# Scores of a head pair in two PSUM banks, and the second FFN matmul three slots later

## The reference

```python
def attn_layer(x, Wqkv, qs, ksc, Wo):            # 16 heads of 64, windows of 32 tokens
    q, k, v = jnp.split(x @ Wqkv, 3, -1)         # each split into heads
    q = l2norm(q) * qs; k = l2norm(k) * ksc      # then rotary, with a scale by position
    sim = jnp.einsum('bhwie,bhwje->bhwij', bq, bk2) * 8.0   # a window against itself and the one before
    attn = jax.nn.softmax(jnp.where(mask, -big, sim), -1)
    return jnp.einsum('bhwij,bhwje->bhwie', attn, bv2) @ Wo

def ffn_layer(x, g, bln, W1, b1, W2, b2):        # inner width 341
    xn = layernorm(x) * g + bln
    a, gate = jnp.split(xn @ W1 + b1, 2, -1)
    return a * gelu(gate) @ W2 + b2

for i in range(6):
    x = attn_layer(shift_tokens(x), ...) + x
    x = ffn_layer(shift_tokens(x), ...) + x
```

## Time and profile before

| | |
|---|---|
| median of 3 runs | 1732.43 us (1731.41 to 1736.98) |
| the profiled execution | 1731.0 us span |
| PE busy | 1639.0 us, 95% |
| DVE busy | 1446.3 us, 84% |
| ACT busy | 1425.6 us, 82% |
| POOL busy | 1311.9 us, 76% |
| DMA | 66.40 MB at 38 GB/s |

### The profile page before, as it was taken

One profiled execution on the slowest core, in us unless ns is written; L12 is line 12 of the kernel. 1 busy time (PEld: TensorE's weight loads), 2 busy tenths in 40 slices (PEclk: granted clock), 3 DMA queues, 4 the chain that ended last, 5 costly groups with the idle time before them and its releaser, 6 DMA issues.

```text
span 1731.0 us, 68758 instructions
## 1 busy us (share of the span) xinstructions
PE 1639.0 (95%) x25970; PEld 1277.2 (74%) x25970; DVE 1446.3 (84%) x3011; ACT 1425.6 (82%) x2851; POOL 1311.9 (76%) x1305
## 2 busy tenths in 40 slices
PE   7779999999999999999999999999999999999995
PEld 5657777777777777777777777777777777777773
DVE  4499888888888888888888888888888888888884
ACT  3367888888888888888888888888888888888885
POOL 6088877877877787787778778787877877777765
PEclk9799999999999999999999999999999999999997
DMA  4111111111111111111111111111111101111000
GB/s 140 41 38 43 35 33 36 30 48 38 41 32 30 36 36 42 49 30 32 30 36 42 49 36 30 32 30 48 38 41 36 30 27 38 35 30 32 28 24 26
DMA packets 41426, 66.40 MB, mean 38 GB/s; under 512 B 7072, under 2 KB 16032, under 8 KB 41376
## 3 DMA queue, kind: packets, MB, share of 16 engines
q1 hardware_dynamic: 40224, 65.38, 12.7%
q10 hardware_dynamic: 1152, 0.34, 0.1%
HBM read 20.61 MB, written 1.05 MB: 13 GB/s over the span
## 4 chain that ended last, share of the span: by engine, by line
PE 61%; ACT 28%; issue 6%; DVE 4%; ACTq 1%; DMA 0%; POOL 0%; DVEq 0%; POOLq 0%
PE ps_qs L530 12%; PE ps_po L530 9%; PE ps_q L530 8%; PE ps_a L530 7%; PE ps_tk L530 7%; PE ps_f L530 6%; PE ps_po L650 5%; ACT p_bd L943 4%; PE ps_k L530 4%; PE ps_v L530 4%; ACT squares L949 4%; ACT L1053 3%; ACT L1050 3%; ACT q_t L943 3%; ACT prob L987 2%
## 5 line engine op out<-in xcount | busy, mean ns | idle before, releaser
L427 POOL TENSOR_TENSOR qk<-qk,rnorm 128x512 f32<-128x512 f32 x384 | 393.6, 1046 | 176.6 <-DVE rnorm L1284 176.1
L419 POOL TENSOR_TENSOR qk<-qk,qk_rot 128x512 f32<-128x512 f32 x384 | 483.8, 1282 | 0.0
L434 POOL TENSOR_TENSOR prob<-prob,row_inv 128x512 f32<-128x512 f32 x192 | 200.7, 1045 | 92.8 <-DVE row_inv L1301 92.8
L1289 DVE TENSOR_REDUCE row_max<-ps_qs 128x8 f32<-128x512 f32 x191 | 132.0, 691 | 164.8 <-PE ps_qs L530 164.8
L943 ACT COPY p_bd<-ps_po 64x512 f32<-64x512 f32 x378 | 219.1, 580 | 58.8 <-PE ps_po L650 56.4
L1264 DVE TENSOR_REDUCE ssq<-squares 128x8 f32<-128x512 f32 x384 | 261.4, 681 | 3.4 <-ACT squares L949 3.4
L530 PEld LDWEIGHTS ps_qs<-k_t,q_t 64*32 64x32 f32 x12224 | 179.2, 107 | 69.0 <-issue 68.9
L943 ACT COPY attn_t<-ps_po 128x512 f32<-128x512 f32 x191 | 112.5, 589 | 133.2 <-PE ps_po L530 133.1
L530 PE MATMUL ps_qs<-k_t,q_t 64*32 64x64 f32 x12224 | 210.1, 218 | 0.0
L530 PE MATMUL ps_po<-p_bd,v_back 128*64 128x64 f32 x3056 | 193.2, 225 | 0.0
L530 PEld LDWEIGHTS ps_po<-p_bd,v_back 128*64 128x64 f32 x3056 | 163.1, 137 | 35.8 <-issue 17.0
(11 more groups left out here) (237 smaller groups left out, 4082.7 us busy)
## 6 DMA issues: line engine op xcount, KB each, us to landing
v_back<-v_own SPq DMA_DIRECT2D x192, 192.0 KB, 2.4
w_raw<-in_wqkv SPq DMA_DIRECT2D x48, 192.0 KB, 2.4
v_back<-v_own SPq DMA_DIRECT2D x96, 64.0 KB, 2.1
wo_sb<-in_wo SPq DMA_DIRECT2D x12, 256.0 KB, 2.9
w_sb<-in_w SPq DMA_DIRECT2D x6, 341.0 KB, 3.1
w_sb<-in_w SPq DMA_DIRECT2D x6, 192.0 KB, 2.7
x_in<-in_x SPq DMA_DIRECT2D x4, 256.0 KB, 4.2
out<-s_out SPq DMA_DIRECT2D x8, 128.0 KB, 1.9
```

The costliest lines, as they stand in the source:

```text
L419: nc.gpsimd.tensor_tensor(qk[:, s, i, :], qk[:, s, i, :], qk_rot[:, s, i, :], ALU.add).then_inc(added, 1)
L427: nc.gpsimd.tensor_tensor(heads(qk[:, s, i, :]), heads(qk[:, s, i, :]), rnorm[:, s, 8 * i:8 * i + 8].unsqueeze(2).to_broadcast([P, 8, HEAD ...
L434: nc.gpsimd.tensor_tensor(heads(prob[:, s, :]), heads(prob[:, s, :]), row_inv[:, s, :].unsqueeze(2).to_broadcast([P, 8, HEAD]), ALU.mult). ...
L1289: V.tensor_reduce(row_max[:, s, :], heads(ps[:]), AX, ALU.max).then_inc(max_done, 1)
```

## The change

Two banks each are taken as one tensor: `ps_qk` is what `ps_q` and `ps_k` were, and `ps_s` is what `ps_qs` and `ps_tk` were. The scores of even heads go to the first 256 columns of the first bank of `ps_s`, those of odd heads to the first 256 columns of the second. The column quarter is now `at = 64 * odd + 32 * low`, with `low` the lower bit of the pair c, and the loops are nested so that eight matmuls that follow each other are on the eight places of the array. Mask, row maximum and subtraction read and write the same 512 elements per partition as 2 x 256, and `p_bd` is indexed to fit. Since the mask now lies over the turned k as well, `lay_mask` waits for `k_turned` too, and both halves of `turn_qk` wait for `sub_done`.

`ff_down` gives up `ps_tk` for `ps_f`, and moves from slot 1 of step n (batch n-4) to slot 0 of step n+1, ahead of `out_projection`. `ln_spread` goes from before `values` to behind it, and waits for the `after_ff` that empties `ps_f`. `after_ff` moves on DVE from the start of slot 2 into slot 0, behind the rotation of k. `load_w2` moves three slots too. The drain is written anew to match.

```diff
-        ps_q, ps_k, ps_v, ps_qs, ps_tk, ps_po, ps_a, ps_f = (
-            bank(n) for n in ("ps_q", "ps_k", "ps_v", "ps_qs", "ps_tk", "ps_po", "ps_a", "ps_f"))
+        ps_qk, ps_s = bank_pair("ps_qk"), bank_pair("ps_s")
+        ps_q, ps_k, ps_qs, ps_tk = ps_qk[:, 0, :], ps_qk[:, 1, :], ps_s[:, 0, :], ps_s[:, 1, :]
+        ps_v, ps_po, ps_a, ps_f = (bank(n) for n in ("ps_v", "ps_po", "ps_a", "ps_f"))
+        def scored(pair):
+            return pair[:, :, 0:OCTET // 2]
...
-                    if b == 3 and j == 2:
+                    if b == 4 and j == 1:
                         load_w2(l)
...
             def turn_qk(u, i, s):
-                ps, read = ((ps_qs, sub_done), (ps_tk, k_turned))[i]
-                wait(pe, read, u)
-                turn_into(ps, u, i, s)
+                wait(pe, sub_done, u)
+                turn_into((ps_qs, ps_tk)[i], u, i, s)
...
-                for c in range(PAIRS):
-                    for half in range(2):
-                        g = 2 * c + half
-                        for odd in range(2):
-                            w = 2 * half + odd
+                for g in range(4):
+                    for odd in range(2):
+                        w = 2 * (g % 2) + odd
+                        for low in range(2):
+                            c = 2 * (g // 2) + low
+                            at = 64 * odd + WINDOW * low
                             for head in range(2):
                                 rows = slice(64 * head, 64 * head + 64)
-                                at = 64 * odd + WINDOW * head
-                                last = mm(ps[at:at + WINDOW, 64 * g:64 * g + 64],
+                                last = mm(pair[at:at + WINDOW, head, 64 * g:64 * g + 64],
...
-            def ln_spread(m, norms):
+            def ln_spread(m, norms, added=0):
                 pe.wait_ge(rnorm_done, norms)
                 wait(pe, ff1_copied, FF_N * m)
+                wait(pe, x_ready, added)
...
-            def ff_down(u, m):
-                pe.wait_ge(k_turned, u + 1)
-                down_into(ps_tk, m)
+            def ff_down(m):
+                wait(pe, ff1_copied, FF_N * (m + 2))
+                down_into(ps_f, m)
...
                         turn_qk(u - 2, 0, j % 2)
-                        if j == 2 and live_batch(n - 4):
-                            pe.wait_ge(x_ready, BATCHES + n - 3)
                         turn_qk(u - 2, 1, j % 2)
                     if j == 0:
+                        if live_batch(n - 5):
+                            ff_down(n - 5)
                         if live_batch(n - 2):
                             out_projection(n - 2, 1)
-                        if live_batch(n - 3):
-                            ln_spread(n - 3, u)
...
-                        if live_batch(n - 4):
-                            ff_down(u - 2, n - 4)
...
                     if live(u - 4):
                         values(u - 4, n - 1, j, j % 2)
+                    if j == 0 and live_batch(n - 3):
+                        ln_spread(n - 3, u, BATCHES + n - 4)
...
             def lay_mask(u, tile):
                 act.wait_ge(q_turned, u + 1)
-                copy(ps_qs[:], mask_b[:, tile, :]).then_inc(mask_laid, 1)
+                act.wait_ge(k_turned, u + 1)
+                copy(scored(ps_s), mask_b[:, tile, :].rearrange("p (a b) -> p a b", a=2)).then_inc(mask_laid, 1)
...
-                    if j == 2 and live_batch(n - 4):
-                        after_ff(n - 4)
...
                     rotate(n, j, 1)
+                    if j == 0 and live_batch(n - 5):
+                        after_ff(n - 5)
                     sum_squares(u, 1, j % 2)
```

More of the change, by code:

```diff
@@ L70, in bank, with bank_pair @@
             return ctx.enter_context(nc.psum_tensor(name, [P, 512], F32))
+        def bank_pair(name):
+            return ctx.enter_context(nc.psum_tensor(name, [P, 2, 512], F32))
         def sem(name):
@@ L355, in _ @@
             with sp.Fori(1, DEPTH - 1) as l:
-                for b in range(4):
+                for b in range(5):
                     body(l * BATCHES + b, b, l)
-                with sp.Fori(4, BATCHES) as b:
+                with sp.Fori(5, BATCHES) as b:
                     body(l * BATCHES + b)
             n = (DEPTH - 1) * BATCHES
-            for b in range(4):
+            for b in range(5):
                 body(n + b, b, DEPTH - 1, slices=False)
-            with sp.Fori(n + 4, STEPS) as n:
+            with sp.Fori(n + 5, STEPS) as n:
                 body(n, slices=False)
@@ L665, in project, with scores @@
                 mm(ps[:], xs_lo[:, toks], w_hi[:, cols], False, True).then_inc(done, 1)
-            def scores(u, j, s, ps=ps_qs, laid=True):
+            def scores(u, j, s, pair=ps_s, laid=True):
                 octet, tile = j // 2, j % 2
@@ L671, in scores @@
                 pe.wait_ge(k_turned, u + 1)
-                if ps is ps_qs and laid:
+                if laid:
                     pe.wait_ge(mask_laid, u + 1)
@@ L827, in drain @@
                 turn_into(ps_q, c, 0, 0)
-                pe.wait_ge(k_turned, c)
-                turn_into(ps_tk, c, 1, 0)
+                pe.wait_ge(k_scaled, END)
+                turn_into(ps_k, c, 1, 0)
                 out_projection(LAST - 1, 1)
-                pe.wait_ge(k_scaled, END)
-                turn_into(ps_k, d, 0, 1)
-                scores(c, 2, 0, ps_q)
+                ff_down(LAST - 4)
+                pe.wait_ge(sub_done, b + 1)
+                turn_into(ps_qs, d, 0, 1)
+                turn_into(ps_tk, d, 1, 1)
+                scores(c, 2, 0, ps_qk, False)
+                values(a, LAST, 0, 0)
+                ln_spread(LAST - 2, END, STEPS + BATCHES - 4)
                 pe.wait_ge(v_copied, END)
-                turn_into(ps_v, d, 1, 1)
-                values(a, LAST, 0, 0)
-                ln_spread(LAST - 2, END)
-                turn_p(b, 1, ps_tk)
+                turn_p(b, 1, ps_v)
                 ln_mean(LAST - 1)
-                pe.wait_ge(sub_done, b + 1)
-                scores(d, 3, 1, ps_qs, False)
+                scores(d, 3, 1, ps_s, False)
                 ff_up(LAST - 2, 0)
@@ L848, in drain @@
                 ff_up(LAST - 2, 2)
-                values(c, LAST, 2, 0, ps_tk)
+                pe.wait_ge(sub_done, c + 1)
+                values(c, LAST, 2, 0, ps_k)
                 out_projection(LAST, 0)
-                turn_p(d, 1, ps_k)
+                turn_p(d, 1, ps_v)
                 ln_spread(LAST - 1, END + 1)
@@ L1108, in drain @@
                 gelu(LAST - 3)
-                keep_p(d, 1, ps_k)
-                keep_attention(c, LAST, 2, ps_tk)
+                keep_p(d, 1, ps_v)
+                keep_attention(c, LAST, 2, ps_k)
                 up_from(ps_f, LAST - 2, 2, ff_pairs[1])
@@ L1285, in newton, with softmax_shift @@
                                        op0=ALU.add, op1=ALU.mult).then_inc(rnorm_done, 1)
-            def softmax_shift(u, s, ps=ps_qs):
+            def softmax_shift(u, s, pair=ps_s):
+                score = scored(pair).rearrange("p a (g k) -> p a g k", k=2 * WINDOW)
+                most = row_max[:, s, :].rearrange("p (a g) -> p a g", a=2)
                 dve.wait_ge(s_done, u + 1)
-                V.tensor_reduce(row_max[:, s, :], heads(ps[:]), AX, ALU.max).then_inc(max_done, 1)
+                V.tensor_reduce(most, score, AX, ALU.max).then_inc(max_done, 1)
                 dve.wait_ge(max_done, u + 1)
                 wait(dve, pt_done, u - 1)
-                V.tensor_tensor(heads(prob[:, s, :]), heads(ps[:]),
-                                row_max[:, s, :].unsqueeze(2).to_broadcast([P, 8, HEAD]),
+                V.tensor_tensor(prob[:, s, :].rearrange("p (a g k) -> p a g k", a=2, k=2 * WINDOW), score,
+                                most.unsqueeze(3).to_broadcast([P, 2, 4, 2 * WINDOW]),
                                 ALU.subtract).then_inc(sub_done, 1)
@@ L1325, in ln_normalise, with after_ff @@
                                        op0=ALU.mult, op1=ALU.mult).then_inc(xn_ready, 1)
-            def after_ff(m, ps=ps_tk):
+            def after_ff(m, ps=ps_f):
                 dve.wait_ge(ff2_done, m + 1)
@@ L1394, in drain @@
                 sums(b, 1)
-                softmax_shift(c, 0, ps_q)
+                after_ff(LAST - 4)
+                softmax_shift(c, 0, ps_qk)
                 ln_normalise(LAST - 2)
@@ L1417, in drain @@
                 newton(END + 1, 1, END)
-                after_ff(LAST - 1)
+                after_ff(LAST - 1, ps_tk)
                 ln_normalise(LAST)
@@ L1423, in drain @@
                 silu_invert(6)
-                after_ff(LAST, ps_f)
+                after_ff(LAST)
                 silu_invert(7)
```

14 lines of the change are left out of this document (8 added, 6 removed).

## The result

| | before | changed |
|---|---|---|
| median | 1734.41 us (4 runs) | 1674.78 us (4 runs) |
| the profiled execution's span | 1731.0 us | 1672.1 us |
| a steady step | 33.63 us | 32.46 us |
| a step of the last layer | 33.63 us | 31.70 us |

The ratio of changed to before is 0.966, with a 95% interval from 0.964 to 0.968: 3.4% faster. 1658 was forecast, with 1620 to 1690 as the range. So sign and range held, and against the 1732.4 from which the forecast started the gain is 58 us where 74 were expected. A step is the distance from one slot's scores to the same slot's of the next step. Of the 59 us between the two spans, the 35 steady steps give 35 x 1.17 = 41, six steps of the last layer 6 x 1.93 = 12, and the unrolled steps and the end the other 6.

What follows compares the result with a forecast made beforehand. PE bound most of the step, with DVE close and ACT's table-load chain; 2.55 us freed on PE less 0.83 us of DVE waits gave 1.72 us a step, 43 steps 74 us: 1658 us, range 1620 to 1690.

Steps and rivals of the forecast that it cites:

- The waits for DVE: PE in slots 2 and 3: of 2.55 us a step that PE gets free, 0.83 us turns into waits for DVE.
- The changes of shape: PE in slot 0: two array-shape changes left of four, about 0.1 us each, so 0.2 us saved.
- The score block: PE's 64 score records: 0.65 us a block in place of 1.02, 0.37 us less in each of four slots.
- The two bounds: Score block between 0.57 us (eight places full) and 1.02 us (start of records already the limit).
- The rule of 25 ns: Matmul starts on PE at least about 25 ns apart, 1.6 us for 64 records; given no weight beyond a rival.
- The chain from slot 0 to slot 2: q projection in slot 1 1.15 us later, ACT's squares +0.98 us; table load and DVE follow, setting slot 2's pace.
- DVE's slot from there to slot 3: DVE needs 7.01 us from slot 2's row maximum to slot 3's, as before the change.
- The mask's wait: ACT's mask waits for `k_turned`: about 0.15 us a unit lost on ACT, 0.4 us cover in slot 1, costed at nothing.
- `ln_spread` waiting for `after_ff`: Slot 0: `after_ff` done by 806.4, spread starts at 806.85; cover 0.5 us, costed at nothing.
- `ff_down` for `ff1_copied`: Slot 0: `ff_down` waits for ACT's copy of the third `ff_up`, between nothing and 1.89 us; taken as nothing.
- The row maximum over 2 x 256: DVE reading 2 x 256: costed at nothing; 0.1 us more per reading would lose 0.4 us in slots 2 and 3.
- eight places are no faster: Rival: score block stays at 1.02 us, the step saves 1.18 us, total 1681 us; chance 0.18.

Runs made afterwards that it cites:

- Changing only POOL's order: Changed kernel with POOL's normalisation of q and k ahead of its weight slice (slot 2) and rounding of x (slot 3): 1658.7 us, repeated 1658.4 us.
- the kernel pinned to four places: Changed kernel with scores on the earlier kernel's four array places, column quarter chosen by head, still two banks: 1695.1 us, step 32.79 us.
- the kernel with the slice in two: Changed kernel, POOL's normalisation first, next layer's weight slice split over slots 0 and 1: 1659.6 us; with heads outermost in the scores as well, 1673.3 us.
- the cut kernel: Changed kernel with the 64 score records in two halves of 32, the four transposes of the probabilities between them: 1732.2 us in a single execution.
- four places for each half of a block: Changed kernel with the loop over the two heads outermost in the scores: 1682.6 us, step 32.62 us, block 0.92 us.

## Why the prediction was right, and where the sum was off

**Right: the places of gain and loss.** No wait of `ff_down`; eight records in a round; ACT's squares of q waiting for PE in slot 1 (0.21 us); new waits of PE for `prob` ahead of turned q. The waits for DVE come to 0.25 + 0.7 = 0.95 us of the steady step; I had 0.83. The last layer's 31.70 us still hold the first of the two, as its PE in slot 2 shows (2.92 us from scores to turned q):

```profile
1501.81 0.86 PE L539 MATMUL ps_s<-k_t,q_t 64*32 64x64 f32 x64
...
1504.73 1.09 PE L539 MATMUL ps_s<-ident,qk 128*128 128x128 f32 x8
```

So PE's own step is about 31.5 us: 33.63 - 0.87 (wait) - 4 x 0.22 (blocks) - 0.4.

**The changes of shape: 0.2 us predicted, 0.38 measured.** From turned q to the projection of q in slot 1 it is 945.18 - 939.63 = 5.55 us, where it was 806.34 - 801.76 = 4.58. So the 1.35 us of `ff_down` make that projection only 0.97 us later, not 1.15.

**The score block: 0.65 us predicted, 0.78 to 0.84 measured.** The two bounds held it. I had taken the whole block near the pace of the rounds; that pace lasts for 32 records. The rule of 25 ns between starts from the Trainium skill, cited in the prediction, does not hold here: eight starts within 0.06 us.

**The chain from slot 0 to slot 2, in time from the turned probabilities of slot 0 (937.73).** Projection of q in slot 1: 7.45 us, 7.63 predicted. Squares: 8.44, 8.60 predicted. Row maximum of slot 2: 16.73, 17.08. Turned q there: 18.19, 18.54. Scores of slot 3: 22.50, 22.80. Up to here the chain is a third of a microsecond better than forecast and otherwise as described: the squares are late by 0.82 us, and what follows is late with them. The third has two parts. About 0.17 us are the shapes. The other 0.19 lie between squares and row maximum, and are the effect of the next paragraph with its sign turned: before, `rn_a` in slot 1 ran into POOL's gate product and took 0.37 us, now it comes clear of it and takes 0.18 (948.58). DVE and POOL of the kernel before:

```profile
809.90 0.37 DVE L1278 SCALAR_TENSOR_TENSOR rn_a<-ssq_c,rn 128x18 f32<-128x18 f32 x1
```

```profile
809.50 0.74 POOL L443 TENSOR_TENSOR ff_m<-ff_a,ff_g 85x256 f32<-85x256 f32 x1
```

**DVE's slot from there to slot 3: 7.01 us predicted, 7.71 measured.** This is the term that was mis-sized, and it turns the gain of 0.3 us into a loss of 0.35: the row maximum of slot 3 stands at 24.44 (24.09), turned q at 25.89 (25.54), the end at 32.46 (31.92; the last 0.19 are 0.15 for the block and 0.04 besides). I took 7.01 from the row maxima of before and kept it, as if DVE's instructions had lengths of their own. But `rnorm` in slot 2 now falls into POOL's slice of weights, and takes 0.98 us in place of 0.18. Changing only POOL's order took that 0.8 away and 18 us off the kernel. The Trainium skill's page "SBUF — State Buffer", section "Who interferes with whom", says that a DVE instruction with two inputs from SBUF contends with a GpSimd instruction that reads SBUF, and that one in a two-port mode and GpSimd shut each other out for a whole instruction. The rows agree, in ends that meet within 0.04 us (0.06 for the clamp).

**The errors together.** 0.15 us in the last block and 0.7 us in DVE, less 0.35 gained in the chain, give 32.46 in place of 31.92. That is 0.54 x 35 = 19 us; the last layer, 0.22 us a step better than predicted, gives 1 back. Everything outside these 41 steps gained 6 us, where the forecast, which had 43 steps at 1.72, gave it 3. So the span is 15 us above the 1657 of the forecast. (The loops run over 42 steps, 5 to 46; the last stands behind them, and the forecast took it with them.) That the total came this near is in part luck: the 0.35 us gained in the chain were not forecast, and by the same sum the step would be that much longer without them.

**Costed at nothing.** The mask's wait: rightly, as far as it was tested. `ln_spread` waiting for `after_ff`: rightly, but the cover is 0.9 - 0.34 = 0.56 us of PE's work, and whoever shortens slot 0 further meets it. `ff_down` for `ff1_copied`: no wait seen. The row maximum over 2 x 256: 0.68 us, as before.

The rival "eight places are no faster" gave 1681 us; the kernel pinned to four places took 1695. A forecast of the step without the blocks was thus 0.33 us too low as well (32.46 against 32.79), of which DVE's `rnorm`, 0.97 us there too, is the named part.

**Still open.** Why only half of a longer block counts in the kernel with the slice in two was read from its slots, not tested; that the last layer shows it too speaks against POOL's slice as the reason, and for PE's wait in slot 2. What slows the second half of a block is not shown either. No kernel reached 31.7 us a step with POOL's slice in it; each place tried for the slice made another short instruction of DVE stand still. The best of them is the one with only POOL's order changed, 1658.4 us, 4.2% under before.

## What to carry to other kernels

The length of a short DVE instruction is not a constant: compare its shortest and longest in the trace, and see whether the long ones end together with an instruction of POOL. When a change shifts DVE against POOL by half a microsecond, the duration has to be worked out anew at the new time. Work of POOL that nobody waits for is best put behind that for which DVE or PE waits, and any move of it is to be followed for the whole step. A block of small matmuls was cheap here for its first 32 records; cut into pieces with other work between, each piece started at the fast pace, but the cut kernel was slower than the whole one (1732 us against 1675), and DVE waits for the block's end.

## What the hardware showed that I had not expected

- Eight 64x32 places, two row halves in one column quarter, run side by side: eight record starts within 0.06 us, 32 within 0.25 us; then a start every 13 ns on average (0.41 us for 32). After the transposes of the probabilities (0.6 us), full speed again.
- With four places for each half of a block, 41 records had started after 0.45 us, and 31 where all were held to four places. This fits only if records of the other half start between those of the first, so that the order of starts between places isn't that of the program; inferred from the counts.
- An 18-element DVE instruction of 0.18 us took 0.58, 0.98 and 1.18 us when it began under a running POOL instruction, and ended with it. So did the one-input clamp (0.18 us alone; 0.47 to 1.15 us).
